# Two of the four tiles of the first layer norm move from ScalarE to GpSimd in a fused cross-attention and expert-routing kernel

## What is computed

```
n  = layernorm(x)                              # "the first norm"
q  = rms_norm_per_head(n @ Wq) * qn_w          # 4 heads of 64
k, v = split(ctx @ Wkv);  k = rms_norm_per_head(k) * kn_w
a  = softmax(q k^T / 8) @ v
x  = x + tanh(g_xattn) * (a @ Wfc + fc_b)
n2 = layernorm(x)                              # "the second norm"
top-2 of 8 experts by n2 @ Wr^T, softmax of the two logits,
capacity 65 tokens per expert and sequence; tokens beyond it are dropped
x  = x + tanh(g_ffn) * sum over both experts of w * (n2 @ We[e])
```

## Time and profile before

| | |
|---|---|
| median of three runs | 1363.23 us (1363.19 to 1363.48) |
| the profiled execution | 1363.08 us, span of its instructions 1361.4 us |
| TensorE matmul busy | 1330.9 us, 98% |
| TensorE weight load busy | 1123.7 us, 83% |
| VectorE busy | 1004.9 us, 74% |
| ScalarE busy | 873.7 us, 64% |
| GpSimd busy | 771.9 us, 57% |
| granted TensorE clock, mean | 0.993 |
| one steady round | 40.76 us |

### The profile page before, as it was taken

How to read it: one execution, slowest core, us unless ns; L and a number is a source line. 1 busy time by engine, 2 the same in 40 slices (tenths; PEclk the granted TensorE clock), 3 DMA queues, 4 the chain that set the end, 5 groups by cost and what they waited for, 6 DMA issues and landing times. The chain is left out here.

```text
span 1361.4 us, 27025 instructions
## 1 busy us (share of the span) xinstructions
PE 1330.9 (98%) x7848; PEld 1123.7 (83%) x7848; DVE 1004.9 (74%) x2959; ACT 873.7 (64%) x2529; POOL 771.9 (57%) x997
## 2 busy tenths in 40 slices
PE   8699999999999999999999999999999999999998
PEld 6678888888888888888888888888888888888876
DVE  6677777777777777777787777787777787777763
ACT  5666676666676666676666676666666666666642
POOL 4445555655555655555655565655565655565644
PEclk9889999999999999999999999999999999999999
DMA  6411112211112211111211112212111211111100
GB/s 199 142 40 57 32 54 62 61 43 58 33 52 62 62 41 58 35 51 61 61 43 59 41 43 62 61 42 61 44 39 61 61 43 59 45 26 47 31 16 24
DMA packets 106835, 73.92 MB, mean 54 GB/s; under 512 B 67776, under 2 KB 85120, under 8 KB 106688
## 3 DMA queue, kind: packets, MB, share of 16 engines
q1 hardware_dynamic: 106688, 72.20, 17.7%
HBM read 40.25 MB, written 31.92 MB: 53 GB/s over the span
## 5 line engine op out<-in xcount | busy, mean ns | idle before, releaser
L382 PE MATMUL bkM<-we,x2T 128*128 128x512 f32 x3072 | 792.4, 401 | 0.9 <-DVE ctx_sb L1264 0.9
L382 PEld LDWEIGHTS bkM<-we,x2T 128*128 128x128 f32 x3072 | 551.8, 188 | 121.0 <-ACT a_out L854 7.5
L854 ACT ACTIVATE a_out<-bkM,gate 128x256 f32<-128x256 f32 x512 | 216.2, 479 | 155.2 <-PE bkM L382 153.9
L1264 DVE SCALAR_TENSOR_TENSOR ctx_sb<-bkM,gate,ctx_sb 128x256 f32<-128x256 f32 x384 | 184.7, 481 | 101.8 <-PE bkM L382 90.2
L632 POOL TENSOR_TENSOR a_sum<-a_sum,a_out 128x256 f32<-128x256 f32 x256 | 188.3, 736 | 119.0 <-ACT a_out L854 87.4
L619 POOL TENSOR_TENSOR probs<-probs,p_inv 128x308 f32<-128x308 f32 x128 | 89.6, 700 | 213.9 <-DVE p_inv L1157 213.9
L573 POOL TENSOR_TENSOR rstd<-ve,minus_half 128x4 f32<-128x4 f32 x64 | 65.1, 1017 | 145.2 <-DVE ve L1048 142.5
L573 POOL TENSOR_TENSOR q_r<-q_ve,minus_half 128x8 f32<-128x8 f32 x64 | 105.3, 1646 | 54.0 <-DVE q_ve L1142 54.0
L731 ACT ACTIVATE xn<-x_sb,shift,rstd 128x256 f32<-128x256 f32 x124 | 64.5, 591 | 77.4 <-DVE shift L1057 77.4
L637 POOL TENSOR_TENSOR ctx_sb<-a_sum,ctx_sb 128x256 f32<-128x256 f32 x128 | 94.8, 740 | 17.0
L815 ACT ACTIVATE probs<-bkA,s_bias,q_r 128x77 f32<-128x77 f32 x128 | 51.4, 412 | 74.0 <-DVE s_bias L1152 74.0
(11 more groups left out here) (202 smaller groups left out, 2583.1 us busy)
## 6 DMA issues: line engine op xcount, KB each, us to landing
x_sb<-in_x SPq DMA_DIRECT2D x32, 512.0 KB, 3.9
out<-ctx_sb SPq DMA_DIRECT2D x64, 256.0 KB, 2.2
v_rows<-v_nat SPq DMA_DIRECT2D x38, 256.0 KB, 2.3
kd<-kT_rows SPq DMA_DIRECT2D x128, 38.5 KB, 2.4
vf<-v_rows SPq DMA_DIRECT2D x128, 38.5 KB
kT_rows<-kT_sb SPq DMA_DIRECT2D x38, 128.0 KB, 2.1
ctx_late<-in_ctx SPq DMA_DIRECT2D x28, 128.0 KB, 3.7
stage<-in_L_ffn_We SPq DMA_DIRECT2D x2, 1024.0 KB, 6.4
```

The lines of the kernel that those rows point to most:

```text
L382: mm = nc.tensor.matmul(out, l, r, start=(i == 0), stop=(i == len(terms) - 1))
L854: ins = nc.scalar.activation(a_out[:, t % 2, (e // 4) * 2 + i], bkM[1][:, i * D:(i + 1) * D], ACT.Copy, scale=gate[:, m.parity, t, e:e + 1])
L1264: nc.vector.scalar_tensor_tensor(out=acc_v[:, t], in0=bkM[0][:, i * D:(i + 1) * D], scalar=gate[:, m.parity, t, e:e + 1], in1=src, op0=ALU ...
```

## The change

`ln1` on ScalarE gets the list of tiles as an argument and in the rounds writes tiles 2 and 3 only. `slots` on GpSimd calls `apply_ln1(f, range(2))` for tiles 0 and 1, behind `finish_tile(m, 0)` and ahead of `ln2(p)`. The two rounds of the fill stay as they are. TensorE still waits for the count of all four tiles.

```diff
@@ -641,6 +641,8 @@
                     ln1(f)
                 if m:
                     finish_tile(m, 0)
+                if f:
+                    apply_ln1(f, range(2))
                 if p:
                     ln2(p)
                 if f and block_of(f):
@@ -723,11 +725,11 @@
             def copy(dst, src, **kw):
                 return nc.scalar.activation(dst, src, ACT.Copy, **kw)
 
-            def ln1(f):
+            def ln1(f, tiles=range(T)):
                 act.wait_ge(shift1_done.sem, shift1_done.at(f))
                 act.wait_ge(xT_ps.sem, xT_ps.before(f))
                 act.wait_ge(qT_ps.sem, qT_ps.before(f))
-                for t in range(T):
+                for t in tiles:
                     nc.scalar.activation(xn1[:, t], x_sb[:, f.parity, t], ACT.Identity,
                                          scale=rstd1[:, t:t + 1], bias=shift1[:, t:t + 1]
                                          ).then_inc(xn1_done.sem, 1)
@@ -871,7 +873,7 @@
                     chunk(k, m, p)
                 if k == 3:
                     if f:
-                        ln1(f)
+                        ln1(f, range(2, T))
                         if block_of(f):
                             kv(block_of(f))
                     chunk(k, m, p)
```

## The result

The changed kernel takes 1368.16 us, the median of six runs (1366.10 to 1368.39), against 1363.36 us (1362.98 to 1364.37) for the kernel before in the same session: a ratio of 1.0033, 95% interval 1.0023 to 1.0044. That is 4.5 us more by the ratio (3.1 to 6.0 by its interval), slower by more than the 0.2% that can be told from nothing. The forecast was 1367.7 us. The profiled execution took 1368.10 us, with a span of 1366.4 us (1363.08 and 1361.4 before).

The account below looks back on a forecast made before the run. TensorE, its matmuls busy 98% of the span, was taken to bound the kernel. Gain 0 and costs 1.1 + 0.4 + 3.0 = 4.5 us on 1363.08 gave 1367.6, the median 0.15 higher: 1367.7 us, range 1365.0 to 1374.0.

Parts of the forecast that it names:

- The bound: TensorE's matmuls are busy 98% of the span; relieving ScalarE pays only where TensorE waits for it: gain 0.
- The price and the start: GpSimd's two tiles take 1.09 us, starting at 665.69 behind finish_tile 0's last add; TensorE's load starts at 666.84.
- Rival 1: GpSimd's tiles slower in a round, 0.74 us each: 14.3 us in all, 1377.5; chance 0.17 in full or half.
- rival 3: GpSimd's tiles quicker in a round than in the fill: 2.5 us, 1365.7; chance 0.03.
- The three kinds of rounds: 27 with a context block lose 0.04 us each, one with TensorE ahead 0.39, two late without context block 1.51 each.
- the sum: Cost over the thirty rounds with a front pair: 1.1 + 0.4 + 3.0 = 4.5 us.
- Moved past: GpSimd's ln2 power starts some 0.9 to 1.1 us later, delaying VectorE's work; xT still reaches q in time: no cost.
- the cover of 0.7 us: Time left between VectorE's low part of xT, ending near 669.86, and TensorE's q at 670.54.
- Rival 2: TensorE catches up at its slot 15 wait, up to 0.5 us per round: 2.0 us, 1365.2; chance 0.14.
- Rival 4: Faster: ScalarE's freed microsecond reaches slot 15's chain, at most 15.2 us less 4.5: 1352.5; chance 0.04.

Follow-up runs that it names:

- ScalarE's relief: Against the kernel before: ScalarE writes tiles 2 and 3 only, nobody writes tiles 0 and 1 in the thirty rounds; 1362.85 us, ratio 0.9999.
- the pair with early gates: Kernel before and changed kernel, each with the first three steps of VectorE's gates moved ahead of pT_part 0 in slot 13; 1353.11 and 1356.41 us.
- its control: The kernel before run again, unchanged; 1363.31 us, ratio 0.9997.
- the two late rounds alone: Against the kernel before: GpSimd writes the two tiles only in the last two rounds with a front pair, without a context block; 1366.91 us, ratio 1.0021.
- the kernel with three tiles: Against the kernel before: GpSimd writes three tiles and ScalarE one, at the place of the change; 1383.43 us, ratio 1.0147.

## Why the prediction was right

**The bound** held. TensorE's matmuls fill 98% of the span in both kernels, and ScalarE's relief by itself is worth nothing (ratio 0.9999).

**The price and the start.** A tile is 555 ns in 64 instructions, where I took the fill's 554; the pair takes 1.09 us, starts 0.01 ahead of the add's end where I had 0.03, and reaches TensorE in 0.05. Rival 1, tiles slowed in a round to 0.74, fell with the group of line 585, whose maximum is 562. So did rival 3, whose tiles would have been quicker than in the fill: the minimum is 546. The Trainium skill ("GPSIMD Engine Reference", 3.1) gives 1.8 cycles per element as a best case, by which I estimated 0.38 us for such a tile; no row here reaches it.

**The three kinds of rounds.** Idle loads were forecast at 0.25 us in a steady round and 1.9 in a late one; the rows show 0.26, and 1.86 and 1.87 in the two late ones. The rounds with a context block cost 1.1 us by the timed runs (1.5 forecast), the late two 2.9 (3.0 forecast), and together these make 4.0 of the 4.5. In the profiled execution itself the steady rounds seem to have cost less: from 96.14 to 1074.10 before and 97.72 to 1075.91 after, 24 rounds grew by 0.23 us, 0.01 each and not 0.04. The list of waits tells why: two of the thirty waits of slot 15 are missing. In these rounds VectorE's den came ahead of GpSimd's add and was not held up, and they took 40.47 and 40.40 us. The other 22 take 40.79 against 40.75: the 0.04 that was forecast. Where those waits are gone in both kernels (the pair with early gates), the steady rounds differ by some 0.06 us.

The two short rounds look like an effect of the change itself, a gain of some 0.7 us that the prediction lacks. All six traces in which GpSimd has one or two tiles more in the steady rounds have only 27 or 28 of the waits of slot 15; the kernel before, its control, ScalarE's relief and the two late rounds alone have all 30, as has the kernel with three tiles. Each is one execution, and why it is always two rounds is open.

**How close the sum is.** The 4.5 us by the ratio are the 4.5 of the sum, but the interval reaches from 3.1 to 6.0, and the trace's rounds grew by 3.53: the sum less the short rounds' 0.7, within 0.3. That the two figures meet to a tenth is luck; the mechanism and its terms are borne out by the rows.

**Moved past.** Right for the steady rounds: VectorE waits 1.16 us for the second norm's rstd (1.1 forecast), and q is not late. What failed is a thing left out: I took the cover of 0.7 us from a steady round and did not work it out for the two late ones, where no k_rsqrt stands behind ln2 and an add of GpSimd holds the shift up. There ln2's delay lengthens a round by some 0.7 us through a late q, as soon as x_transpose is on time. In the changed kernel it is hidden behind the 1.5 us of lateness at x_transpose, which is why the sum did not suffer.

**The rivals.** Rival 2, that TensorE catches up in slot 15, was weighed at 0.14. Three tiles decided it: 20.0 us, against 6 to 12 if it had caught up. Rival 4 fell with ScalarE's relief.

## What to carry to other kernels

Moving work off an engine that nobody waits for gains nothing, and what it costs is decided at one point: when the last of the moved pieces is ready, against when the bounding engine could start. Work that point out for each kind of round, the rare ones too, since two rounds of thirty held about two thirds of the cost here; and look at what is queued behind the moved work in those rounds as well, since a larger wait may hide a second one. If the bounding engine's own list of waits has an entry in nearly every round, start there: three tiny instructions on VectorE, moved into a gap in which it waited, brought 9 us.

## What the runs showed of the hardware

- A weight load may start late without loss as long as the matmul ahead covers it. With two tiles the idle time before it grew by 0.21 us (0.05 to 0.26), and an undisturbed steady round by 0.04; with three tiles it grew by 0.74, and the round by 0.56. So 0.17 to 0.19 us were free, where the prediction had 0.16.
- Some of VectorE's small instructions take 0.4 to 0.7 us in place of 0.13 to 0.19 when a GpSimd instruction on SBUF has begun before them, and end within some 0.05 us of it. In the kernel before these are the `tensor_scalar` ones with their operand in SBUF (ve, den) and those with two inputs in SBUF (gap, w_top, g_all, the late shift). Others run beside the adds at full speed: the batch-norm aggregate (0.16 us with or without), the sums over q_sq (0.69) and the additions to the chunk, whose other input is in PSUM (0.48). The Trainium skill ("GPSIMD Engine Reference", 8) names contention with VectorE instructions of two SBUF inputs or in a two-port mode. The rows agree for those with two inputs; den and ve read one, and no run shows in which mode they ran. GpSimd is not slowed: in the changed kernel its tiles stay within 546 and 562 ns.
- Which of the two starts first is a matter of hundredths of a microsecond. The first norm's shift, which starts within 0.01 us of a GpSimd add, keeps its 0.13 us, and a round with den ahead of the add is 0.3 to 0.4 us shorter. The fill varies by 2 us. The kernel before lay between 1359.76 and 1365.02 us in 33 runs; how this spread divides I did not settle.
